# A graph network of six convolutions on one core: the one-hots of a ring's last two edge tiles move to GpSimd, and two small edits

## The chip, the cores and the metric

The kernel runs on one core of a Trainium2 chip. The time is the device time of one execution in microseconds (us), lower is better. One core has five engines that run their own instruction streams and wait for each other by semaphores: TensorE (PE, its weight loads are shown as PEld), VectorE (DVE), ScalarE (ACT), GpSimd (POOL) and SyncE (SP, which here issues nearly all DMAs).

## The reference, cut to what matters

There are 1250 nodes with 512 features and 20000 edges, sorted by dst. Four residual blocks follow one another; each normalizes x, applies a relu, and aggregates over the edges. With them there are six convolutions, called L0, L1A, L1B, L2, L3A and L3B in the kernel.

```python
edge_index = jnp.stack([src, dst])
h = jnp.maximum(_layernorm(x, axis=-1), 0.0)
x = x + relu(mean_of_neighbours(h) @ L0_W_l.T + L0_b_l + h @ L0_W_r.T)           # L0
h = jnp.maximum(_layernorm(x, axis=-1), 0.0)
x = x + sage(relu(sage(h, L1_W1l, L1_b1, L1_W1r)), L1_W2l, L1_b2, L1_W2r)        # L1A, L1B
h = jnp.maximum(_layernorm(x, axis=-1), 0.0)
x = x + layernorm(h + relu(h @ W_self.T + b_self + mean(h[dst] @ W_neigh.T + b_neigh))) * gamma + beta   # L2
h = jnp.maximum(_layernorm(x, axis=-1), 0.0)
x = x + gcn(relu(gcn(h, L3_W1, L3_b1)), L3_W2, L3_b2)                            # L3A, L3B
```

Every aggregation is a sum over the same edges. It can therefore be written as a product with one 1250 x 1250 matrix of edge counts, and that is what the kernel does.

## The kernel before, in words

The nodes are cut in 10 tiles of 128 (NT). The kernel first builds the matrix of counts on TensorE, and then uses it in every convolution.

**Counting, 13 to 138 us.** The edges come in tiles of 128. For a tile, `src_hot` (128 edges x 640) and `dst_hot` (128 edges x 128) are one-hot matrices, 1 where the edge's node equals the column, and the product of the two, summed over edge tiles, is a block of the count matrix. The count matrix is made in 20 windows: b from 0 to 9 and half h from 0 to 1. As the edges are sorted by dst, a window needs only some edge tiles. How many is read at run time from a table (`tiles_of`, through `visits_of`), rounded up to a multiple of RING = 6. One pass over a ring of six edge tiles is called a trip here. Low nodes have more edges, so the first windows take more trips. Each half has its own ring of buffers, `src_hot[h]` and `dst_hot[h]`, with six slots.

In a trip the work is split by slot e:

- DVE (`givers`, line 1197) writes all six `src_hot` (line 1212), and the `dst_hot` of the slots e with BY_ACT <= e < RING - 1, which is slot 4 alone (line 1210). Before slot e it awaits `hot_used[h] >= n + e + 1`, that is, that PE has used this slot in the trip before.
- ACT (`receivers`) writes the `dst_hot` of slots 0 to 3 in two steps: the distance of node and column (`apart`, line 800), then the relu of one minus the distance (line 806).
- GpSimd (`last_receivers`, line 594) writes the `dst_hot` of slot 5. Per window it copies the window's table row into `tab_now` (line 597). Per trip it copies the nodes of the edges in its slot into `key_now` (line 602), awaits that copy, awaits `hot_used[h] >= n + RING`, that is, that PE has used all six slots of the trip before, writes the one-hot (line 607), and awaits its own result.
- PE (`count`, line 1684) multiplies slot by slot, two matmuls of 128 x 320 for each (line 1700), so 12 for a trip. It awaits `first_rows` at slots 0 and 2, `last_rows` at slot 5 and `givers_ready` at each slot, and increments `hot_used` after each slot. Two small matmuls with zeros open a window (line 1690) and one closes it (line 1705). ACT then moves the counts out of PSUM (line 771).

Between the windows PE runs the products of L0: a tile of normalized x is turned (line 1714) and multiplied by the two weights, 12 matmuls each (line 1721, `first_p` and `first_q`). The order on every engine is written out by hand: `merged(b, r)` is followed by `merged_end(b, r)`. For b of 2 to 7 PE has this in a loop of three rounds with two b in each; GpSimd has a loop over b with both halves in it.

**Statistics.** In this stage DVE also makes the mean and variance of a tile of x: `statistics_1` (bn_stats, line 1184), `statistics_2` (bn_aggr into `mv_now`, line 1189) and `statistics_3` (line 1193), a multiplication by 1.0 that moves `mv_now` into the column of `mv` that belongs to the tile.

**The convolutions, from 138 us on.** In each, PE makes the products of the 10 tiles (`products`, line 1721), and then aggregates for 10 receivers i: 20 matmuls of count columns with p_hi and p_lo (line 1814). ACT casts the count columns for receiver i + 2 (`stage`, line 844) when PE is through with receiver i, and DVE combines the result (line 1436), adds it to x, and makes the statistics and the normalized tile of the next convolution. From L1A on these tiles are turned by way of DRAM: DVE transposes 32 x 32 blocks (`square`), SP writes them out (`park`) and reads them back turned into `zT` (`turn`, line 515). ACT makes hT_hi of such a tile (`hi`, line 828), DVE hT_lo (`lo`, line 1236).

ACT works in order, so an `hi` that stands between two casts holds up the second until its DMA has landed. At the end of a convolution, `receive_all` on ACT puts the `hi` of the next convolution's tiles 0 and 1 behind the casts at receivers i = 5 + late // 2 and 6 + late // 2, where late is 2 ahead of L2 and 0 otherwise; DVE has its `lo` at the same i.

```python
def receive(i, staged):
    if staged:
        stage(s, i + 2, i % 2)
    if s + 1 in NORMED:
        deviation(NORMED[s + 1], i)
```

## Time and profile before

| | |
|---|---|
| median of 3 runs | 646.88 us (646.28 to 648.64) |
| profiled execution | 647.0 us |
| span of its trace, first to last instruction | 645.1 us |
| busy: PE / DVE / ACT / POOL | 97% / 62% / 47% / 13% of the span |
| mean granted TensorE clock | 0.997 of full speed |

The profiled execution and the median agree within 0.1 us, so sums made on the trace can be held against the median. The rows that follow come from the profile's page and from views of the trace. Times are us from the start of the span unless marked ns. A row of a group of instructions gives the line, engine, operation, output and inputs and how many there are, then the time busy and the mean of one in ns, then how long the engine sat idle before them and what ended that. A row of a timeline gives the start, the duration, the engine and the line; several instructions in a row are merged in one, with their number behind x, and in square brackets stands the idle time before and what ended it. Matmuls overlap in their records, so the time between the starts says more than a duration.

### The profile page before, as it was taken

The numbers are of one execution on the slowest core, as the hardware profiler recorded it, in microseconds if no ns is written. First come the engines' busy times: TensorE is split into PE (matmuls) and PEld (weight loads), VectorE is DVE, ScalarE is ACT, GpSimd is POOL, SyncE is SP. The second block draws the span as 40 slices with busy tenths as digits, with TensorE's granted clock in tenths as the row PEclk, the third lists the DMA queues.
The fourth block names the chain that finished last, engine by engine and source line by source line (L and its number), as shares of the span: only waits on it lengthen the run. The fifth ranks groups of instructions, "written<-read, shape, count | busy, mean of one in ns | idle before, by whom it ended". The sixth has DMA issues, their size and how long they took to land.

```text
span 645.1 us, 11113 instructions
## 1 busy us (share of the span) xinstructions
PE 626.6 (97%) x3047; PEld 511.2 (79%) x3048; DVE 401.5 (62%) x875; ACT 303.8 (47%) x628; POOL 85.2 (13%) x135
## 2 busy tenths in 40 slices
PE   5989999999989999999999999999999999999997
PEld 4547767777868888888888888888888998899886
DVE  6998999977867434533434888754999730531222
ACT  4887886644423454431224342225478752565210
POOL 4442433200000000000000000000354070000000
PEclk9999999999999999999999999999999999999999
DMA  6300005457684422587550465431200000000102
GB/s 215 117 1 2 1 23 80 63 125 150 105 172 109 109 33 72 142 207 173 122 91 6 130 142 148 98 65 49 81 1 1 1 2 1 2 0 1 49 17 97
DMA packets 151843, 48.39 MB, mean 75 GB/s; under 512 B 133500, under 2 KB 137396, under 8 KB 151800
## 3 DMA queue, kind: packets, MB, share of 16 engines
q1 hardware_dynamic: 150520, 45.34, 30.8%
q10 hardware_dynamic: 1280, 2.56, 1.2%
q8 instruction: 17, 0.28, 0.2%
q14 instruction: 26, 0.21, 0.1%
HBM read 30.44 MB, written 17.44 MB: 74 GB/s over the span
## 4 chain that ended last, share of the span: by engine, by line
PE 86%; DVE 4%; DMA 3%; issue 2%; SPq 2%; ACT 1%; DVEq 1%; ACTq 0%
PE ps L1721 33%; PE ps L1814 23%; PE ps L1851 13%; PE ps L1877 8%; PE ps L1700 8%; DMA count_rows<-count_squares 2%; SPq L491 1%; DVE src_hot L1212 1%; DMA wstage<-in_L_gnn_W_l 1%; PE ps L1714 1%; DVE stats L1184 1%; DVE p_lo L1504 0%; ACT cstage L844 0%; DMA zT<-rows 0%; DVE own L1436 0%
## 5 line engine op out<-in xcount | busy, mean ns | idle before, releaser
L1814 PE MATMUL ps<-p_hi,cstage 128*128 128x512 f32 x400 | 156.0, 390 | 2.8 <-ACT cstage L844 2.8
L1814 PE MATMUL ps<-p_lo,cstage 128*128 128x512 f32 x400 | 155.7, 389 | 0.0
L1721 PE MATMUL ps<-w_hi,hT_hi 128*128 128x512 f32 x320 | 126.3, 395 | 0.6 <-issue 0.4
L1721 PE MATMUL ps<-w_hi,hT_lo 128*128 128x512 f32 x320 | 124.7, 390 | 0.0
L1721 PE MATMUL ps<-w_lo,hT_hi 128*128 128x512 f32 x320 | 124.6, 389 | 0.0
L1814 PEld LDWEIGHTS ps<-p_hi,cstage 128*128 128x128 f32 x400 | 75.1, 188 | 19.7 <-ACT cstage L844 2.9
L1814 PEld LDWEIGHTS ps<-p_lo,cstage 128*128 128x128 f32 x400 | 75.1, 188 | 15.5
L1212 DVE TENSOR_SCALAR src_hot<-iota,nodeT 128x640 bf16<-128x640 f16 x210 | 69.0, 384 | 5.8 <-PE ps L1700 3.7
L1700 PE MATMUL ps<-src_hot,dst_hot 128*128 128x320 bf16 x420 | 65.7, 305 | 5.8 <-DVE src_hot L1212 2.9
L1721 PEld LDWEIGHTS ps<-w_hi,hT_hi 128*128 128x128 f32 x320 | 60.1, 188 | 13.3 <-issue 0.9
L1721 PEld LDWEIGHTS ps<-w_hi,hT_lo 128*128 128x128 f32 x320 | 60.1, 188 | 12.7
L1721 PEld LDWEIGHTS ps<-w_lo,hT_hi 128*128 128x128 f32 x320 | 60.1, 188 | 11.9
L1700 PEld LDWEIGHTS ps<-src_hot,dst_hot 128*128 128x128 bf16 x420 | 36.9, 99 | 28.7 <-DVE src_hot L1212 12.9
L844 ACT CAST cstage<-countT 128x1280 fp32r<-128x1280 uint16 x30 | 37.6, 1263 | 42.7 <-PE ps L1814 40.0
L653 POOL TENSOR_TENSOR x<-x,vec 128x512 f32 (+1 forms) x10 | 13.8, 1387 | 320.8 <-ACT relued L849 320.8
L833 ACT ACTIVATE p_hi<-ps 128x512 fp32r<-128x512 f32 (+1 forms) x40 | 23.8, 596 | 64.5 <-PE ps L1721 64.4
L1242 DVE TENSOR_TENSOR p_lo<-ps,p_hi 128x512 fp32r<-128x512 f32 x40 | 27.5, 689 | 41.7 <-ACT p_hi L833 41.6
L1599 DVE TENSOR_TENSOR u_lo<-ps,u_hi 128x384 fp32r<-128x384 f32 (+1 forms) x24 | 12.5, 585 | 59.3 <-ACT u_hi L957 59.3
L1436 DVE SCALAR_TENSOR_TENSOR own<-ps,nodal,own 128x512 f32<-128x512 f32 x40 | 29.5, 737 | 28.9 <-PE ps L1814 28.9
L946 ACT CAST spans<-countT 128x384 fp32r<-128x384 uint16 (+1 forms) x60 | 31.7, 552 | 33.1 <-PE ps L1851 32.8
L800 ACT ACTIVATE apart<-tab,nodeT 128x128 bf16<-128x128 f16 (+1 forms) x140 | 44.6, 392 | 1.6 <-ACT dst_hot L806 0.4
L1851 PE MATMUL ps<-spans,p_hi 128*128 128x384 f32 (+1 forms) x120 | 42.2, 352 | 0.9 <-issue 0.7
(156 smaller groups left out, 941.3 us busy)
## 6 DMA issues: line engine op xcount, KB each, us to landing
rows<-squares SPq DMA_DIRECT2D x38, 256.0 KB, 2.5
zT<-rows SPq DMA_DIRECT2D x120, 64.0 KB, 2.5
count_rows<-count_squares SPq DMA_DIRECT2D x10, 320.0 KB, 2.2
countT<-count_rows SPq DMA_DIRECT2D x40, 80.0 KB, 3.2
x<-in_x ACTq DMA_DIRECT2D x1, 2304.0 KB
out_x<-x SPq DMA_DIRECT2D x9, 256.0 KB
wstage<-rows SPq DMA_DIRECT2D x32, 64.0 KB, 2.5
wstage<-in_L_gnn_W SPq DMA_DIRECT2D x2, 1024.0 KB, 5.7
```

The lines of the kernel that those rows point to most:

```text
L800: nc.scalar.activation(apart[h][:, e:e + 1, :], tab[:, window(b, h), :], ACT.Abs, scale=-1.0, bias=nodeT[:, 0, bass.ds(t + e, 1)]).then_in ...
L833: nc.scalar.activation(p_hi[:, bass.ds(i, 1), :], ps[:, p_bank(s, r), :], ACT.Copy, scale=1.0 if CONVS[s]["own"] else dis[:, bass.ds(i, 1) ...
L844: nc.scalar.copy(stage_of(s, r), columns(s, i)).then_inc(stage_ready, 1)
L946: nc.scalar.copy(span_of(n % SLOTS, n), span_counts(n)).then_inc(span_ready, 1)
L1212: nc.vector.tensor_scalar(src_hot[h][:, e, :], iota[:, :], nodeT[:, 1, bass.ds(t + e, 1)], None, ALU.is_equal).then_inc(givers_ready[h], 1)
L1242: nc.vector.tensor_tensor(p_lo[:, bass.ds(i, 1), :], ps[:, p_bank(s, r), :], p_hi[:, bass.ds(i, 1), :].bitcast(F32), ALU.subtract).then_in ...
L1436: nc.vector.scalar_tensor_tensor(own_, ps[:, AGG + r:AGG + r + 1, :], scale[:, bass.ds(i, 1)], own_, ALU.mult, ALU.add).then_inc(t_done, 1)
L1700: last = nc.tensor.matmul(ps[:, COUNT + 2 * h + k, 0:NS // 2], dst_hot[h][:, e, :], src_hot[h][:, e, k * (NS // 2):(k + 1) * (NS // 2)], s ...
L1721: last = nc.tensor.matmul(ps[:, bank, :], a[:, r, k, :], w[:, slot, k, :], start=n == 0, stop=n == len(pairs) - 1)
L1814: last = nc.tensor.matmul(ps[:, AGG + r, :], cstage[:, part, k, :], p_[:, k, :], start=n == 1, stop=n == 2 * len(parts) * NT)
L1851: last = nc.tensor.matmul(ps[:, u_bank(l, g) + f, 0:cols], h[:, k, f * P:(f + 1) * P], spans[:, c, 0:cols], start=k == 0 and m == 0, stop= ...
L1877: last = nc.tensor.matmul(ps[:, dense_bank(l, i), :], u[g % 2][:, k, own_], w[:, 0, k, :], start=m == 0, stop=m == len(pairs) - 1)
```

## The change

GpSimd writes the dst_hot of slots 4 and 5, one instruction each, from a key_now of two columns. It still awaits hot_used once for the trip. DVE then writes no dst_hot at all, since BY_ACT <= e < RING - BY_POOL holds for no slot. PE awaits `last_rows` at slot 4 and, with a higher value, at slot 5. The statistics of the counting stage go from bn_aggr to their place in mv directly. And the hi and lo of the next convolution's first two tiles stand at 5 + (s != L1A) and 6 + (s != L1A) where they stood at 5 + late // 2 and 6 + late // 2: for s = L0 that is 6 and 7 where it was 5 and 6; for L1A (5 and 6) and L1B (6 and 7) it is what it was.

```diff
-    BY_ACT = 4
+    BY_ACT, BY_POOL = 4, 2
...
-    mv_now, _ = place("mv_now", [P, 2], F32)
...
-    key_now, _ = place("key_now", [P, 1], F32, place.end)
+    key_now, _ = place("key_now", [P, BY_POOL], F32, place.end)
...
-                    nc.gpsimd.tensor_copy(key_now[:, :], nodeT[:, 0, bass.ds(t + RING - 1, 1)]
+                    nc.gpsimd.tensor_copy(key_now[:, :], nodeT[:, 0, bass.ds(t + RING - BY_POOL, BY_POOL)]
                                           ).then_inc(key_set[h], RING)
                     pool.wait_ge(key_set[h], n + RING)
                     pool.sem_inc(passed_pool, 1)
                     pool.wait_ge(hot_used[h], n + RING)
-                    nc.gpsimd.tensor_scalar(dst_hot[h][:, RING - 1, :], tab_now[:, :], key_now[:, 0:1], None,
-                                            ALU.is_equal).then_inc(last_rows[h], RING)
+                    for k in range(BY_POOL):
+                        nc.gpsimd.tensor_scalar(dst_hot[h][:, RING - BY_POOL + k, :], tab_now[:, :], key_now[:, k:k + 1],
+                                                None, ALU.is_equal).then_inc(last_rows[h], RING // BY_POOL)
                     pool.wait_ge(last_rows[h], n + RING)
...
# ACT, receive_all
-                        if i == 5 + late // 2:
+                        if i == 5 + (s != L1A):
                             first_tile(0)
-                        if i == 6 + late // 2:
+                        if i == 6 + (s != L1A):
                             first_tile(1)
...
# DVE
-                statistics_3(v, i)
...
-                nc.vector.bn_aggr(mv_now[:, :], stats[:, :]).then_inc(aggr_done, 1)
-
-            def statistics_3(v, i):
-                dve.wait_ge(aggr_done, NT * v + i + 1)
-                nc.vector.tensor_scalar(mv[:, bass.ds(i, 1), :], mv_now[:, :].unsqueeze(1), 1.0, None,
-                                        ALU.mult).then_inc(mv_done, 1)
+                nc.vector.bn_aggr(mv[:, i, :], stats[:, :]).then_inc(mv_done, 1)
...
-                        if BY_ACT <= e < RING - 1:
+                        if BY_ACT <= e < RING - BY_POOL:
...
-                        if i == 5 + late // 2:
+                        if i == 5 + (s != L1A):
                             lo(s + 1, 0, 0)
-                        if i == 6 + late // 2:
+                        if i == 6 + (s != L1A):
                             lo(s + 1, 1, 1)
...
# PE, count
-                        if e == RING - 1:
-                            pe.wait_ge(last_rows[h], n + RING)
+                        if e >= RING - BY_POOL:
+                            pe.wait_ge(last_rows[h], n + (e + 1 - (RING - BY_POOL)) * RING // BY_POOL)
```

## Rows read from the trace of the kernel before

**Rows 1.** The page: busy tenths of the span in 40 equal slices.
```profile
PE   5989999999989999999999999999999999999997
...
DVE  6998999977867434533434888754999730531222
```

**Rows 2.** Groups of instructions, 13 to 47.2 us.
```profile
L1700 PEld LDWEIGHTS ps<-src_hot,dst_hot 128*128 128x128 bf16 x156 | 13.1, 102 | 18.5 <-DVE src_hot L1212 11.7 <-issue 1.4 <-POOL dst_hot L607 1.1
L607 POOL TENSOR_SCALAR dst_hot<-tab_now,key_now 128x128 bf16<-128x128 f16 x13 | 11.4, 879 | 8.1 <-PE ps L1700 6.7 <-POOL key_now L602 1.4
...
L1210 DVE TENSOR_SCALAR dst_hot<-tab,nodeT 128x128 bf16<-128x128 f16 x13 | 3.3, 253 | 0.2 <-PE ps L1700 0.2
```

**Rows 3.** Timeline of GpSimd in the first stretch: start, duration, what, idle before.
```profile
22.50 0.19 POOL L602 COPY key_now<-nodeT 128x1 f32 x1 [0.61 <-POOL dst_hot L607]
...
22.96 0.91 POOL L607 TENSOR_SCALAR dst_hot<-tab_now,key_now 128x128 bf16<-128x128 f16 x1 [0.27 <-PE ps L1700]
...
24.95 0.91 POOL L607 TENSOR_SCALAR dst_hot<-tab_now,key_now 128x128 bf16<-128x128 f16 x1 [0.27 <-PE ps L1700]
...
28.05 0.83 POOL L607 TENSOR_SCALAR dst_hot<-tab_now,key_now 128x128 bf16<-128x128 f16 x1 [0.27 <-POOL key_now L602]
...
45.41 0.81 POOL L607 TENSOR_SCALAR dst_hot<-tab_now,key_now 128x128 bf16<-128x128 f16 x1 [0.71 <-PE ps L1700]
```

**Rows 4.** Timeline of DVE: src_hot beside a GpSimd one-hot, and without.
```profile
23.03 1.91 DVE L1212 TENSOR_SCALAR src_hot<-iota,nodeT 128x640 bf16<-128x640 f16 x6
...
61.27 1.28 DVE L1212 TENSOR_SCALAR src_hot<-iota,nodeT 128x640 bf16<-128x640 f16 x4 [0.72 <-PE ps L1700]
```

**Rows 5.** Waits, total, times, longest: 13 to 47.2 us, then 91 to 131.
```profile
POOL dst_hot L607 <- PE ps L1700: 6.7, 8, 1.8
...
POOL dst_hot L607 <- PE ps L1700: 10.8, 6, 2.4
```

**Rows 6.** Timeline of GpSimd in the second stretch and after it.
```profile
62.55 0.93 POOL L607 TENSOR_SCALAR dst_hot<-tab_now,key_now 128x128 bf16<-128x128 f16 x1 [2.25 <-PE ps L1700]
...
65.97 1.30 POOL L607 TENSOR_SCALAR dst_hot<-tab_now,key_now 128x128 bf16<-128x128 f16 x1 [0.27 <-POOL key_now L602]
...
68.76 0.93 POOL L607 TENSOR_SCALAR dst_hot<-tab_now,key_now 128x128 bf16<-128x128 f16 x1 [0.55 <-PE ps L1700]
...
109.98 0.60 POOL L607 TENSOR_SCALAR dst_hot<-tab_now,key_now 128x128 bf16<-128x128 f16 x1 [2.37 <-PE ps L1700]
```

**Rows 7.** Timeline of GpSimd before the counting: two iotas in a row.
```profile
1.22 0.28 POOL L573 IOTA tile_up<- 128x162 f32 x1
1.45 0.28 POOL L575 IOTA tile_dn<- 128x162 f32 x1
```

**Rows 8.** Timeline of PE: counting matmuls, and those that close a window (L1705).
```profile
26.20 0.19 PE L1705 MATMUL ps<-zeros 128*128 128x64 bf16 x1
...
47.12 0.19 PE L1705 MATMUL ps<-zeros 128*128 128x64 bf16 x1
...
60.58 3.42 PE L1700 MATMUL ps<-src_hot,dst_hot 128*128 128x320 bf16 x24
63.84 0.19 PE L1705 MATMUL ps<-zeros 128*128 128x64 bf16 x1
...
93.02 2.20 PE L1700 MATMUL ps<-src_hot,dst_hot 128*128 128x320 bf16 x12
```

**Rows 9.** Timelines of ACT and PE around 184 us.
```profile
184.04 0.63 ACT L828 ACTIVATE hT_hi<-zT 128x512 fp32r<-128x512 f32 x1 [3.67 <-DMA zT<-rows]
184.57 1.24 ACT L844 CAST cstage<-countT 128x1280 fp32r<-128x1280 uint16 x1
...
186.15 0.47 PE L1814 MATMUL ps<-p_hi,cstage 128*128 128x512 f32 x1 [2.48 <-ACT cstage L844]
```

**Rows 10.** The chain of work that ended last: start, us, what; one receiver of L0.
```profile
147.12 4.83 PE ps L1814 x20
```

More of the change, by code:

```diff
@@ L243, in gnn_kernel @@
     coarse_set, exact_set, fine_set = sem("coarse_set"), sem("exact_set"), sem("fine_set")
-    aggr_done = sem("aggr_done")
     scaled_done = sem("scaled_done")
@@ L1305, in _ @@
             statistics_2(0, 0)
-            statistics_3(0, 0)
             split_first(1, range(0, 2))
@@ L1312, in _ @@
             statistics_2(0, 1)
-            statistics_3(0, 1)
             givers(1, 1, found)
@@ L1320, in _ @@
             statistics_2(0, 2)
-            statistics_3(0, 2)
             lo(L0, 1, 1)
@@ L1338, in merged_end @@
                 statistics_2(0, b + 1)
-                statistics_3(0, b + 1)
                 lo(L0, b, r)
```

## Prediction, made before the changed kernel was run

> **What bounds the kernel now.** I read the slices of the span first, then the groups of instructions, the waits of GpSimd, and the timelines of PE and GpSimd. The slices show PE at nine tenths or more from the fifth slice on (one slice dips just after the first), and DVE at seven tenths or more in slices 2 to 11 [rows 1]. So after about 48 us only what makes PE wait counts; before that PE waits for one-hots. The change touches the counting stage (13 to 138 us) and one stretch at 184 us.
>
> In the first 34 us of counting there are 13 trips of the ring, one GpSimd one-hot each. PE's weight loads sat idle 11.7 us until DVE had a src_hot ready and only 1.1 us until GpSimd [rows 2]. This invites the reading "DVE is the bound, GpSimd has room". Its second half has to be tested: GpSimd's one-hots take 11.4 us of the 34, but it also idles around each of its own small copies, and that is no room. Between two one-hots of one window lie 0.61 us until key_now starts, 0.19 of key_now and 0.27 until the one-hot starts: 1.07 [rows 3]. With 0.91 for the one-hot the loop needs 1.98 us a trip, and from 22.96 to 24.95 is 1.99: GpSimd is as close to the limit there as DVE, whose six src_hot take 1.91 and whose dst_hot comes on top [rows 3, 4]. From the last one-hot of a window to the first of the next it needs 28.05 - 25.86 = 2.19 us [rows 3].
>
> Real room is only what GpSimd waited for PE: 6.7 us in 8 waits [rows 5], less the 0.27 that lie before a one-hot in any case, also where nothing from PE is awaited (28.05) [rows 3]: 6.7 - 8 x 0.27 = 4.5 us over 13 trips, or 0.35 a trip.
>
> **What the second one-hot costs GpSimd.** The trace has no two in a row. A lone one, with DVE writing no one-hot at the time, spans 0.60 [rows 6]; beside src_hot the spans are 0.91 and 0.93 [rows 3, 6]; with a DVE dst_hot beside it too, one took 1.30 [rows 6]. Two iotas back to back span 0.28 each but start 0.23 apart [rows 7], so the spacing may be 0.05 less than a span. Bounds: 0.55 and 0.93. In the first stretch I take 0.78, between the ends, since a longer ring trip leaves DVE idle for part of the second one-hot. The wider key_now (two columns for one) is taken at its present 0.19; bounds 0 and 0.05 more a trip, inside those of the one-hot.
>
> **First stretch, 13 to 47 us.** Added are 13 x 0.78 = 10.1 us, less the room of 4.5: GpSimd's last one-hot ends 5.6 later. That one ended at 46.22, and PE's closing matmul came at 47.12, 0.90 behind, because DVE was later still [rows 3, 8]. With GpSimd as the bound, the distance is that of the first window: 25.86 to 26.20, 0.34 [rows 3, 8]. So PE ends **5.6 - 0.6 = 5.0 us later**. With 0.55 it is 7.2 - 4.5 - 0.6 = 2.1; with 0.93, and 0.5 of the room unusable where PE itself is slow (its longest wait was 1.8 [rows 5]), it is 12.1 - 4.0 - 0.6 = 7.5. What DVE saves, 13 dst_hot of 0.25 us [rows 2] and the copies of statistics, buys nothing once GpSimd is the bound. The work of DVE and ACT between windows ends before GpSimd's pair does, since they are through with the last trip's slots before GpSimd begins its second one-hot.
>
> **Second stretch, 47 to 91 us: six windows of two trips.** PE runs 24 matmuls in 3.26 us (60.58 to 63.84, 0.136 each) without a stop [rows 8], trip 2's slots being filled while it eats trip 1's. After the change slots 4 and 5 are both written only once PE has used slot 5 of trip 1, since hot_used is awaited once, for the whole trip. Now the one-hot starts at 62.55 and PE's closing matmul at 63.84, 1.29 later [rows 6, 8]. After: 0.93 + 0.65 + 0.34 = 1.92, **0.63 more**. The second is taken at 0.65 here, near the lone 0.60, because DVE's last src_hot of the window end under the first and statistics follow; with 0.93 it is 0.91 more, with 0.85 and 0.55 it is 0.45 more. Six windows make 3.8. In the two after the loop's turn GpSimd itself will be late for trip 2: before 68.76 it had 0.55 - 0.27 = 0.28 us of room, after a one-hot of 1.30 [rows 6], against about 0.8 added and 0.1 less for want of the dst_hot beside it; I take 0.35 each, bounds 0 and 0.5. Sum **+4.5 us**, bounds 2.7 and 6.5.
>
> **Ten windows of one trip, 91 to 138 us.** GpSimd waited 10.8 us in 6 waits for PE there [rows 5]: 9.2 of room, against 10 second one-hots of 0.6 to 0.9, so PE covers them: 0, at worst 1 us. In the first of these windows 12 matmuls took 2.20 us [rows 8], where 3.42 - 12 x 0.136 = 1.79 is the time without a stop; DVE was late, and with a dst_hot and a copy less (some 0.4 us) this goes: **-0.4 us**. Statistics written straight into mv are off PE's path everywhere else: 0.
>
> **The turned tiles' move.** Only L0's receiving stage changes: ACT's hT_hi of L1A's tile 0 (and DVE's lo) moves from receiver 5 to 6, tile 1's from 6 to 7; for L1A and L1B the old and the new expression agree. ACT waited 3.67 us for the tile's DMA, until 184.04, with the cast of the counts for receivers 8 queued behind (184.57, 1.24 us); PE sat idle 2.48 us for that cast, until 186.15 [rows 9]. After the move the cast starts where that wait began, at 184.04 - 3.67 = 180.37, and ends by 181.7, two us ahead of PE's need at 183.67. Next on ACT's queue behind tile 0's turn is now the cast for receivers 9, from 184.7 to 186.0, and PE wants it after receiver 8's 20 matmuls, which take 4.8 us in the chain [rows 10], so at about 188. SP's order is unchanged. So **-2.5 us**. The lo of tile 0 also no longer holds up DVE; but its transposes for the next tiles then wait more on their DMAs, which may come back as a stop in L1A's products: bounds -2.5 and -1.0.
>
> **Sum** on the profiled execution: 5.0 + 4.5 - 0.4 - 2.5 = +6.6 us, so 647.0 + 6.6 = **653.6 us** (a span of 645.1 with 1.9 around it). The median of the runs, 646.88, differs from it by 0.1. Low ends: 2.1 + 2.7 - 0.4 - 2.5 = +1.9, 648.9. High ends: 7.5 + 6.5 + 1.0 - 0.4 - 1.0 = +13.6, 660.6.
>
> **Rules of the Trainium skill against these rows.** Where six src_hot run with a GpSimd one-hot beside them they take 1.91 us (from 23.03), 0.318 each; four with GpSimd idle take 1.28 (from 61.27), 0.32 each, while GpSimd's own span is 0.91 instead of 0.60 [rows 3, 4, 6]. So GpSimd is held up and DVE is not. The Trainium skill ("SBUF — State Buffer", section "Who interferes with whom") says that a DVE operation in a two-port mode and a GpSimd operation lock each other out, whoever starts second waiting for the whole of the other. The trace agrees on GpSimd's side only; what the other side would give is the rival of that name below. The Trainium skill ("Perfetto Trace Analysis", section "GPSIMD Engine Instruction") also holds that GpSimd's spans are unreliable and that start-to-start spacing is to be used; with the iotas' difference that moves the sum toward its low end.
>
> **Rivals.**
> *GpSimd's room suffices, and the kernel gets faster.* DVE would then stay the bound of the first stretch and lose 13 x 0.25 = 3.3 us: 647.0 - 3.3 - 0.4 - 2.5 = 640.8. For it: the 11.7 us against 1.1 [rows 2]. It decides if the second one-hot takes GpSimd less than 0.35 us of its loop; the shortest row is 0.60. Chance 0.07.
> *The short spacing.* Everything as in my sum with the low ends: 648.9, within 0.5%. For it: the iotas [rows 7], and a DVE that idles more. With cases between it and 650.2 I give it 0.18.
> *Long one-hots.* GpSimd stays beside src_hot all the time, 0.93 or more, and the move's gain is partly given back: 660.6 at the end, 657 in the middle. For it: the 1.30 us that one one-hot took [rows 6], should it be src_hot and not DVE's dst_hot that stretched it. Chance 0.20.
> *DVE is locked out too.* Then a trip costs DVE 6 x 0.318 + 2 x 0.60 = 3.1 us against 2.75 in my GpSimd loop (1.07 + 0.90 + 0.78): 25 x 0.35 = 8.8 more, 662.4. Against it: rows 4. Chance 0.03.
> *The move does nothing* (the wait for turned tiles shows up on PE at the next stage): 656.1. Chance 0.07.
> *My sum*, 651 to 656: 0.45.
>
> **Numbers.** 0.5%, 3.2 us, is about what a measurement of this kernel can tell from no change (its three runs span 2.4 us). Faster than 643.6 takes the first rival: 0.07. Within: 0.18. Slower than 650.2: 0.75. The range leaves out the first rival, what lies beyond the low end and the last 1.6 us before the high end, with DVE locked out: 648.6 to 659.
>
> **What would show it.** In the changed profile: two one-hots in a row per trip on GpSimd, and PE's idle time in counting released by GpSimd instead of DVE; the start-to-start time of first one-hots near 2.75 instead of 1.99 in the first window; counting windows with two trips of some 3.9 us instead of 3.26 on PE; PE without the 2.48 us before the cast of columns 8. The forecast is wrong if two one-hots take GpSimd under 1.3 us, if DVE's src_hot gets longer than 0.38 on average, or if PE stops at the start of L1A's products.

## The result, and the profile after

| | before | after |
|---|---|---|
| median (runs in this comparison) | 646.96 us (7) | 650.91 us (7) |
| extent of the runs | 645.45 to 648.64 | 649.90 to 651.21 |
| profiled execution, its span | 647.0, 645.1 | 651.15, 649.2 |

The ratio is 1.0056, with an interval of 1.0041 to 1.0070: **slower by 4.0 us**, where 6.6 were forecast. It lies in the range, on the side given 0.75.

The page of after first: busy tenths in 40 slices (PE, then DVE), then groups of instructions, then the shares of the chain that ended last.

```profile
PE   6879999999999999999999999999999999999997
...
DVE  6887779877887534443434788754989730541222
...
L1689 PE MATMUL ps<-src_hot,dst_hot 128*128 128x320 bf16 x420 | 69.6, 307 | 9.1 <-POOL dst_hot L606 5.8
...
L1205 DVE TENSOR_SCALAR src_hot<-iota,nodeT 128x640 bf16<-128x640 f16 x210 | 67.9, 387 | 15.5 <-PE ps L1689 13.2
...
L606 POOL TENSOR_SCALAR dst_hot<-tab_now,key_now 128x128 bf16<-128x128 f16 x70 | 51.6, 747 | 20.6 <-PE ps L1689 16.8
...
PE 90%; POOL 4%; DVE 2%; issue 1%; DMA 1%; ACT 1%; ACTq 1%; SPq 0%; DVEq 0%; POOLq 0%
```

DVE is less busy in the first slices than in [rows 1], and now it is PE that DVE waits for: 13.2 us before src_hot. Of the 9.1 us that PE itself idles before its counting matmuls, GpSimd ends 5.8. The mean of a GpSimd one-hot is 747 ns, and there are 70, two for each of 35 trips.

The waits over the whole span in after (total us, times, longest):

```profile
PE ps L1689 <- POOL dst_hot L606: 5.8, 17, 1.2
...
PEld ps L1689 <- DVE src_hot L1205: 14.4, 26, 1.5
...
PEld ps L1689 <- POOL dst_hot L606: 8.3, 18, 0.6
```

The weight loads still seem to wait most for DVE. This is the trap of [rows 2] again, the other way round: DVE itself waits for PE, 13.2 us in the group above, so it isn't what closes the circle. That is seen on the engine that waits for nobody. That is GpSimd, in its timeline of after (start, duration, what, in brackets the idle time before):

```profile
16.95 1.56 POOL L606 TENSOR_SCALAR dst_hot<-tab_now,key_now 128x128 bf16<-128x128 f16 x2 [1.60 <-PE ps L1689]
...
22.14 1.49 POOL L606 TENSOR_SCALAR dst_hot<-tab_now,key_now 128x128 bf16<-128x128 f16 x2 [0.27 <-PE ps L1689]
24.24 0.19 POOL L600 COPY key_now<-nodeT 128x2 f32 x1 [0.61 <-POOL dst_hot L606]
24.69 1.49 POOL L606 TENSOR_SCALAR dst_hot<-tab_now,key_now 128x128 bf16<-128x128 f16 x2 [0.27 <-PE ps L1689]
...
49.34 1.18 POOL L606 TENSOR_SCALAR dst_hot<-tab_now,key_now 128x128 bf16<-128x128 f16 x2 [0.27 <-PE ps L1689]
...
66.64 1.56 POOL L606 TENSOR_SCALAR dst_hot<-tab_now,key_now 128x128 bf16<-128x128 f16 x2 [1.26 <-PE ps L1689]
```

From 22.14 to 24.69 is 2.55 us, where one trip took 1.99 in [rows 3]: the same 1.07 around GpSimd's own copy, and 1.49 for two one-hots in place of 0.91 for one. The 0.27 before each pair is the time that also stands there when nothing is awaited, so GpSimd has no room left in these trips. At 66.64, in the second trip of a window, it does wait for PE.

Where the time went, by stages. The first matmul of counting, the closing matmuls of windows (b, h) and the first aggregation of L0 are starts in PE's timeline:

| start of | before | after | shift |
|---|---|---|---|
| counting | 13.67 | 13.40 | -0.27 |
| closing matmul of (0,0) | 26.20 | 28.76 | +2.56 |
| closing matmul of (1,1) | 47.12 | 50.86 | +3.74 |
| closing matmul of (4,1) | 90.05 | 97.54 | +7.49 |
| closing matmul of (5,0) | 95.05 | 102.16 | +7.11 |
| L0's aggregation | 147.12 | 154.14 | +7.02 |
| L1A's products | 195.55 | 199.59 | +4.04 |
| end of the span | 645.1 | 649.2 | +4.1 |

One thing in the first of these shifts is not the change. In most executions TensorE's granted clock is at the lower of its two levels (1.2 in place of 2.4 GHz) for part of the first microseconds of counting, and its counting matmuls then start 0.27 us apart instead of 0.136. Counting matmuls between 15 and 17 us, in before, in after and in c_after, which is the changed kernel as the experiments have it (us, PE busy with their number, granted clock, DMA share, GB/s):

```profile
15.00:17.00 2.00, 2.00 (x9) 0.50 1.03 392
15.00:17.00 2.00, 2.00 (x9) 1.00 1.05 401
15.00:17.00 2.00, 1.84 (x13) 1.00 1.03 390
```

After has 9 of them as before has, although its row says 1.00; its record of the clock begins only at 17.7 us. From the first to the twelfth start, the matmuls of the first trip take 2.11 us in before, 2.90 in after and 1.50 in c_after.

PE in the second stretch and at the windows' ends in after, which answers to [rows 8]:

```profile
50.86 0.19 PE L1694 MATMUL ps<-zeros 128*128 128x64 bf16 x1
...
64.67 2.88 PE L1689 MATMUL ps<-src_hot,dst_hot 128*128 128x320 bf16 x20
...
67.75 0.95 PE L1689 MATMUL ps<-src_hot,dst_hot 128*128 128x320 bf16 x4 [0.20 <-POOL dst_hot L606]
68.53 0.19 PE L1694 MATMUL ps<-zeros 128*128 128x64 bf16 x1
...
97.54 0.19 PE L1694 MATMUL ps<-zeros 128*128 128x64 bf16 x1
...
100.53 1.79 PE L1689 MATMUL ps<-src_hot,dst_hot 128*128 128x320 bf16 x12
```

The 24 matmuls that ran in 3.26 us before are now broken behind the twentieth, and take 68.53 - 64.67 = 3.86. The twelve of the first one-trip window run in 1.79 us, without their old stop.

ACT in L0's last receivers of after, which answers to [rows 9]:

```profile
187.29 1.25 ACT L843 CAST cstage<-countT 128x1280 fp32r<-128x1280 uint16 x1
...
190.85 0.62 ACT L827 ACTIVATE hT_hi<-zT 128x512 fp32r<-128x512 f32 x1
191.37 1.25 ACT L843 CAST cstage<-countT 128x1280 fp32r<-128x1280 uint16 x1
```

The turned tile's hi no longer waits for its DMA at all, and PE runs through.

### The profile page after: what moved, and what is told of

It is laid out like the page before. It is cut to its first block, busy times and chain, and to the rows that moved or that the text cites. A ratio compares the mean times of both kernels' runs of the same rounds, so it can differ in the third digit from the quotient of the medians.

```text
span 649.2 us, 11033 instructions
## 1 busy us (share of the span) xinstructions
PE 630.0 (97%) x3047; PEld 511.5 (79%) x3048; DVE 394.8 (61%) x830; ACT 304.3 (47%) x628; POOL 106.4 (16%) x170
## 3 DMA queue, kind: packets, MB, share of 16 engines
q10 hardware_dynamic: 1280, 2.56, 1.2%
## 4 chain that ended last, share of the span: by engine, by line
PE 90%; POOL 4%; DVE 2%; issue 1%; DMA 1%; ACT 1%; ACTq 1%; SPq 0%; DVEq 0%; POOLq 0%
PE ps L1710 33%; PE ps L1803 27%; PE ps L1840 13%; PE ps L1866 8%; PE ps L1689 7%; POOL dst_hot L606 4%; PE ps L1703 1%; DMA wstage<-in_L_gnn_W_l 1%; DVE p_lo L1493 0%; PE ps L1661 0%; DVE own L1453 0%; ACTq L425 0%; PE ps L1679 0%; ACT cstage L843 0%; DVE stats L1182 0%
## 5 line engine op out<-in xcount | busy, mean ns | idle before, releaser
L1689 PE MATMUL ps<-src_hot,dst_hot 128*128 128x320 bf16 x420 | 69.6, 307 | 9.1 <-POOL dst_hot L606 5.8
L1205 DVE TENSOR_SCALAR src_hot<-iota,nodeT 128x640 bf16<-128x640 f16 x210 | 67.9, 387 | 15.5 <-PE ps L1689 13.2
L1710 PEld LDWEIGHTS ps<-w_hi,hT_hi 128*128 128x128 f32 x320 | 60.1, 188 | 13.2 <-issue 0.7
L843 ACT CAST cstage<-countT 128x1280 fp32r<-128x1280 uint16 x30 | 37.6, 1263 | 42.7 <-PE ps L1803 40.0
L606 POOL TENSOR_SCALAR dst_hot<-tab_now,key_now 128x128 bf16<-128x128 f16 x70 | 51.6, 747 | 20.6 <-PE ps L1689 16.8
```

The source lines that it names most:

```text
L606: nc.gpsimd.tensor_scalar(dst_hot[h][:, RING - BY_POOL + k, :], tab_now[:, :], key_now[:, k:k + 1], None, ALU.is_equal).then_inc(last_rows ...
L843: nc.scalar.copy(stage_of(s, r), columns(s, i)).then_inc(stage_ready, 1)
L1205: nc.vector.tensor_scalar(src_hot[h][:, e, :], iota[:, :], nodeT[:, 1, bass.ds(t + e, 1)], None, ALU.is_equal).then_inc(givers_ready[h], 1)
L1689: last = nc.tensor.matmul(ps[:, COUNT + 2 * h + k, 0:NS // 2], dst_hot[h][:, e, :], src_hot[h][:, e, k * (NS // 2):(k + 1) * (NS // 2)], s ...
L1710: last = nc.tensor.matmul(ps[:, bank, :], a[:, r, k, :], w[:, slot, k, :], start=n == 0, stop=n == len(pairs) - 1)
```

## The experiments

Two bases carry the experiments. In them and in all that follow, the loaded entry of the table has a stated range, which puts two more instructions of each engine's sequencer in front of a window:

```diff
-            tiles_of[0:1, window(b, h)], engines=[engine.engine], bass_reorder=False)
+            tiles_of[0:1, window(b, h)], engines=[engine.engine], bass_reorder=False,
+            min_val=0, max_val=65535)
```

All ratios are to the kernel before without this line, run on the same chip, with 95% intervals. "First" is the stretch from the first counting matmul to the closing of (1,1), "second" from there to the closing of (4,1), and "receivers" from L0's first aggregation to L1A's products. The three are of one profiled execution each.

| kernel | median, us | ratio | first | second | receivers |
|---|---|---|---|---|---|
| before | 646.96 | 1 | 33.45 | 42.93 | 48.43 |
| after | 650.91 | 1.0056 [1.0041, 1.0070] | 37.46 | 46.68 | 45.45 |
| c_before | 651.09 | 1.0028 [1.0008, 1.0048] | 34.27 | 42.90 | 50.98 |
| c_after | 654.65 | 1.0091 [1.0060, 1.0122] | 38.05 | 46.79 | 45.42 |
| e1_one_hot_back | 645.83 | 0.9956 [0.9938, 0.9974] | 34.76 | 42.77 | 45.44 |
| e2_gpsimd_alone | 659.05 | 1.0155 [1.0118, 1.0193] | 38.86 | 46.84 | 52.21 |
| e3_move_alone | 645.64 | 0.9987 [0.9967, 1.0007] | 35.31 | 42.88 | 45.44 |
| e4_added_alone | 657.78 | 1.0177 [1.0136, 1.0219] | 38.74 | 46.61 | 49.21 |
| e5_slot_4_left_out | 646.68 | 0.9992 [0.9968, 1.0016] | 32.22 | 42.85 | 49.91 |
| e6_wait_for_each | 652.10 | 1.0096 [1.0062, 1.0131] | 38.36 | 46.01 | 45.44 |
| g1_stop_filled | 649.67 | 1.0011 [0.9992, 1.0030] | 34.96 | 43.06 | 49.52 |
| g3_none_on_gpsimd | 646.70 | 0.9964 [0.9942, 0.9985] | 34.91 | 42.72 | 45.44 |
| g4_two_from_third_block | 649.96 | 1.0016 [0.9996, 1.0037] | 32.71 | 47.05 | 45.44 |

Two cautions. The kernel before was timed anew beside each group of experiments (its median was 646.74 us beside one group and 648.99 beside another), so kernels are compared by their ratios. And the first stretch varies by 1 us and more from one execution to the next, mostly by how long PE counts at the lower clock: the matmuls of the first trip take 1.50 us in c_after and g4, 2.0 to 2.5 in before, c_before, e1, e2, e4, e5, e6 and g3, 1.73 and then 2.81 for the second trip in g1, and 2.90 in after and e3, where e3 has 2.67 for the second trip too. With one one-hot on GpSimd, from c_before, e3 and e1, the stretch is 34.27, 35.31 and 34.76. From the closing of (0,0) to that of (1,1), behind that start, it is 21.11, 21.11 and 21.73. The second stretch lies between 42.7 and 43.1 us in every kernel with at most one one-hot on GpSimd and between 46.6 and 47.1 in those with two and one wait, and the receivers without a stop at 45.42 to 45.45, so these are the sharper instrument.

**The two bases.**

> The kernel before, with a range assertion behind each load of a window's table entry (two sequencer instructions on each engine per window), which all experiments have; it is the base for them. The assertions lie between windows, 20 times. If PE is the bound there (after 48 us) they hide; before it four windows may pay 0.1 to 0.2 us each on DVE. Expected 647.0 to 648.0 us.

> The changed kernel with the same assertions. If they cost both kernels the same, it is 4.0 us above c_before, 651 to 652. As GpSimd is on the path between windows until 98 us, its assertions may cost a little more here: up to 5 us above c_before. In the trace: closing matmul of the last two-trip window about 7.5 us later than in c_before.

The stated range costs about 0.3% in each, 1.8 us in c_before where 0 to 1 was expected. The change costs 1.0091 against 1.0028 between them, so its effect is about the same as without the range (1.0056), and the second stretch and the receivers of c_after repeat those of after. The first stretch is 0.6 longer than in after, for two reasons that pull apart: up to the closing of (0,0) it is 1.2 shorter, as PE had the full clock in the first trip, and from there to the closing of (1,1) it is 23.87 us against 22.10. There GpSimd's added instructions lie on its path between windows (from its last pair in (0,0) to the first in (0,1) it needs 2.72 us, from 27.69 to 30.41, where after has 2.38; e2, e4 and e6, with the range too, have 23.75 to 24.02 for the whole), and the granted clock fell once more, from 43.2 to 46.6 us.

**One one-hot given back.** All of the change but its first part:

```diff
-    BY_ACT, BY_POOL = 4, 2
+    BY_ACT, BY_POOL = 4, 1
```

> The changed kernel with BY_POOL = 1: DVE makes slot 4's one-hot again, the move and the statistics stay. Theory (GpSimd's second one-hot is the whole loss, the move the whole gain): PE's closings of the windows fall back to those of before, 7.0 to 7.4 us earlier than in c_after, the move's 3.0 us stays: 3.0 to 3.2 us below c_before, about 644. Rival (the pair costs little by itself and the move or the statistics cost something in the counting): less than 5 us below c_after.

The second stretch falls back from 46.79 to 42.77 us and the first from 38.05 to 34.76. The ratio is 1.3% below c_after's and 0.44% below the kernel before, so the second one-hot on GpSimd is what the change loses by. This version is faster than both, even with the range on it. Against c_before it gains 5.3 us where 3.0 to 3.2 were expected: c_before's receivers took 5.5 us more than e1's, and not 3.0, since its stop of PE was longer and the clock fell behind it.

**GpSimd's part alone, on the kernel before.** The hunks for GpSimd, for PE's waits and for DVE's slot 4 from the change; statistics and the turned tiles stay as they were.

```diff
-                        if BY_ACT <= e < RING - 1:
+                        if BY_ACT <= e < RING - BY_POOL:
...
-                        if e == RING - 1:
-                            pe.wait_ge(last_rows[h], n + RING)
+                        if e >= RING - BY_POOL:
+                            pe.wait_ge(last_rows[h], n + (e + 1 - (RING - BY_POOL)) * RING // BY_POOL)
```

> The kernel before with the GpSimd part alone (slots 4 and 5 on GpSimd), no move, statistics as before. Theory: 7.0 to 7.4 us above c_before, about 654.3; PE's stop of 2.5 us ahead of receiver 8 of L0 is there again. Rival (the loss hangs on the statistics or the move together with it): below 652.

First +4.6 and second +3.9 us against c_before, as forecast within the spread of the first stretch. The time rose by 1.3%, some 8 us, because the receivers also took 1.2 us more than in c_before; the section on the hardware comes back to that.

**The move alone, on the kernel before.**

```diff
-                        if i == 5 + late // 2:
+                        if i == 5 + (s != L1A):
...
-                        if i == 6 + late // 2:
+                        if i == 6 + (s != L1A):
```

> The kernel before with only the move: hi and lo of L1A's first two tiles one receiver later. Theory: PE starts L1A's products 2.5 to 3.0 us earlier and nothing gives it back: about 644.3. Rival (the transposes for the next tiles then wait for their DMAs and stop PE in L1A's products): 646 to 647, with an idle PE before L1721 after 200 us.

The receivers take 45.44 us, the value of every kernel with the move, with no stop of PE there nor at the start of L1A. The ratio falls from 1.0028 to 0.9987, or 0.41% (about 2.7 us; the two intervals just fail to touch). The rival that the stop would come back in the next stage is refuted.

**GpSimd's added time alone.** GpSimd writes a second one-hot into a buffer that nobody reads; DVE keeps slot 4, and PE has its old waits.

```diff
+                    nc.gpsimd.tensor_scalar(spare[:, :], tab_now[:, :], key_now[:, 0:1], None,
+                                            ALU.is_equal).then_inc(last_rows[h], RING // 2)
                     nc.gpsimd.tensor_scalar(dst_hot[h][:, RING - 1, :], tab_now[:, :], key_now[:, 0:1], None,
-                                            ALU.is_equal).then_inc(last_rows[h], RING)
+                                            ALU.is_equal).then_inc(last_rows[h], RING // 2)
```

> The kernel before in which GpSimd makes one further one-hot per trip, into a spare buffer that nobody reads, ahead of its own; DVE still makes slot 4's. It separates what GpSimd pays from what DVE saves. Theory (GpSimd's time is the bound, what DVE saves is worth nothing): as e2, 7 us above c_before, 654. If DVE's saving counts, or the two engines hold each other up: 656 to 658, and src_hot on DVE longer than its mean of 385 ns. If PE's further wait at slot 4 is what costs: it isn't there in this kernel, and the time is near 648.

First +4.5 and second +3.7 against c_before; e2 had +4.6 and +3.9. So the loss needs neither PE's wait at slot 4 nor the missing dst_hot of DVE: GpSimd's time alone makes it. The time itself, 657.78 us, is above the 654 of the theory and within the 656 to 658 of its rival, and src_hot did get longer, 392 ns from 13 to 92 us against c_before's 386. But e2, in which DVE is relieved, has the same two stretches and 390 ns, and its ratio, 1.0155, has an interval that overlaps e4's. If the two engines hold each other up, DVE's part of it is those 6 ns for each src_hot. What DVE saves in e2 is worth nothing that can be seen in these two stretches once GpSimd is the bound.

**Nobody writes slot 4.** On the kernel before. The buffer is filled with zeros once at the start, so the edges of slot 4 are missing from the counts.

```diff
-                        if BY_ACT <= e < RING - 1:
+                        if False:
```

> The kernel before in which nobody makes slot 4's one-hot (it holds zeros from the start, so the edges of slot 4 are left out of the counts); GpSimd makes slot 5's only. It shows what relieving DVE is worth when GpSimd isn't charged for it. The rival of the prediction priced it at 13 x 0.25 = 3.3 us. Theory: GpSimd's loop of 1.98 us in the first window and ACT's of 1.95 stand next to DVE's, so only the starts of windows gain: 1 to 2.5 us below c_before, plus 0.3 at the first one-trip window.

This is the most that the change could have brought by relieving DVE: the first stretch 2.05 us shorter, the second 0.05, the time 0.36% (2.3 us). The rival, 13 x 0.25 = 3.3 us, asked for too much: with one one-hot GpSimd's loop is itself at 1.98 us a trip, and it takes over after the first microseconds won. In e5 no one-hot of GpSimd from 20.98 us to the end of the stretch waits longer than the 0.27 that are always there.

**A wait for each slot.** On c_after: GpSimd awaits slot 4 and slot 5 one by one, and so may begin the pair before PE has used slot 5.

```diff
-                    pool.wait_ge(hot_used[h], n + RING)
                     for k in range(BY_POOL):
+                        pool.wait_ge(hot_used[h], n + RING - BY_POOL + 1 + k)
```

> The changed kernel in which GpSimd awaits slot 4's own release (hot_used of n + 5) before the first one-hot and slot 5's before the second, instead of slot 5's release before both. Theory: in the six two-trip windows after 51 us PE releases GpSimd, so the pair starts 0.27 us earlier (two matmuls) in each: 1.6 us below c_after. In the first four windows GpSimd goes straight from its key to the pair, and nothing changes. Rival (the single wait is the fault of the whole loss): 4 us or more below c_after.

A miss. The second stretch is 0.78 us shorter, half of what was expected, and the ratio is c_after's (1.0096 and 1.0091). The first is 0.31 longer, but that is the clock of its start: from the closing of (0,0) on it is 23.75 us against 23.87. GpSimd's timelines tell why; the same pair first in c_after, then in e6:

```profile
67.66 1.56 POOL L607 TENSOR_SCALAR dst_hot<-tab_now,key_now 128x128 bf16<-128x128 f16 x2 [0.80 <-PE ps L1690]
```

```profile
67.52 1.63 POOL L607 TENSOR_SCALAR dst_hot<-tab_now,key_now 128x128 bf16<-128x128 f16 x2 [0.78 <-PE ps L1690]
...
21.84 1.42 POOL L607 TENSOR_SCALAR dst_hot<-tab_now,key_now 128x128 bf16<-128x128 f16 x2 [0.33 <-PE ps L1690]
```

The pair is longer by 0.07 (the second wait stands inside it), and where GpSimd is the bound the start costs 0.33 in place of 0.27; a trip there still takes 2.54 us, against 2.55 in c_after. The 0.27 us that PE takes over a slot's two matmuls are all that the earlier start can win, and the two waits give back about half of them: 0.78 us over six windows is 0.13 for each.

**None on GpSimd.** On c_after with BY_POOL = 0: GpSimd's part of counting and PE's wait for it are left out, and DVE writes slots 4 and 5.

> The changed kernel with BY_POOL = 0: DVE makes the one-hots of slots 4 and 5, GpSimd none. With e1 (one on GpSimd) and c_after (two) it gives the third point. Theory (with one on GpSimd the two engines are level): DVE is the bound and pays 0.17 to 0.25 us more a trip: the first four windows take 2 to 3 us more than in e1, the six two-trip windows 0 to 1 more; 648 to 650 us. Rival (GpSimd's one-hot already costs more than it saves): the same as e1 or faster, 643 to 646.

A miss too. The second stretch is 42.72 us against e1's 42.77, the first 34.91 against 34.76, and the ratios are 0.9964 and 0.9956. The loss inside a window is there, in DVE's timeline of g3:

```profile
22.61 1.27 DVE L1180 TENSOR_SCALAR src_hot<-iota,nodeT 128x640 bf16<-128x640 f16 x4 [0.16 <-PE ps L1662]
...
24.96 1.27 DVE L1180 TENSOR_SCALAR src_hot<-iota,nodeT 128x640 bf16<-128x640 f16 x4 [0.16 <-PE ps L1662]
```

A trip takes 2.35 us there. With one one-hot on GpSimd and the range it is 2.13 (in c_before and e1, while [rows 3] have 1.99 without the range), so DVE pays 0.22 us more a trip, as expected. But it pays them only in the first window: that one takes 13.71 us against c_before's 13.16, and the three windows after it 21.20 against 21.11. What evens that out is open. From a window's closing matmul to the first counting matmul of the next, the three together take 6.46 us against 6.65, so GpSimd's path from one window to the next is worth 0.2 at most.

e1, on the other side, lost time to a single one-hot in window (0,1). GpSimd's row and the matmul of PE that waited for it:

```profile
32.14 3.03 POOL L607 TENSOR_SCALAR dst_hot<-tab_now,key_now 128x128 bf16<-128x128 f16 x1 [1.47 <-PE ps L1690]
...
35.23 2.34 PE L1690 MATMUL ps<-src_hot,dst_hot 128*128 128x320 bf16 x14 [1.54 <-POOL dst_hot L607]
```

The one-hot spans 3.03 us, to just behind the end of an unbroken run of DVE's instructions from 30.7 to 35.0, and PE idles 1.54 us for it. g1 has the same one at 32.23. Without it e1's first stretch would be shorter, by 1.5 us at most, so GpSimd's first one-hot may be worth 1 to 2 us; the times don't show it.

**Two one-hots from the third block on.** On c_after: GpSimd writes one for b = 0 and 1 and two from b = 2, DVE and PE accordingly.

```diff
+            with pool.Fori(0, 2) as b:
+                for h in range(2):
+                    last_receivers(b, h, 1)
-            with pool.Fori(0, NT) as b:
+            with pool.Fori(2, NT) as b:
...
+                by_pool = 1 if isinstance(b, int) and b < 2 else BY_POOL
```

> The changed kernel with one one-hot on GpSimd in the first four windows and two from the fifth on. It separates the two stretches. Theory (two separate losses that add up): the first stretch falls to that of e1, 3.3 us less than c_after (GpSimd's loop no longer the bound), the second stays at 46.7 to 46.8 us against 42.8 (the pair behind PE's release); 651 us. Rival (the first stretch's delay is what makes the second late): the second stretch falls too, near 43 to 45 us.

The first stretch is that of one one-hot (32.71; 20.63 from the closing of (0,0), against 21.11 in c_before), the second that of two (47.05). The two losses are separate and add up; the one in the second stretch is not the first one carried on. The first stretch is the shortest of all kernels that have one one-hot there and count fully, since in this execution the clock was full from the start. The ratio is 0.7% below c_after's and still above e1's.

**The stop filled.** On c_before: in front of the aggregation for L0's receiver 8, where PE idles, it gets 12 matmuls into a free part of PSUM whose product nobody uses.

```diff
+                        if s == L0:
+                            for _ in range(12):
+                                nc.tensor.matmul(ps[:, COUNT, :], p_hi[:, 0, 0:P], p_hi[:, 0, :],
+                                                 start=True, stop=True)
                         aggregate(NT - 2, 0, parts(0))
```

> c_before, in which PE, ahead of receiver 8 of L0, makes 12 matmuls of 512 columns whose result nobody uses (2.7 us). Without them PE idles there for 2.5 to 3.8 us until ACT's cast, and in c_before, e2, e4 and e5 the granted clock fell to 0.6 to 0.8 of full in the slices right behind, which made L0's receivers take 49.2 to 52.2 us (45.4 with the move). Theory (the move is worth more than the stop, since the idle PE also loses clock): the clock stays at 1.0 behind the stop and the receivers take 45.4 + 3.0 to 4.2 = 48.4 to 49.6 us; time 1 to 2 us below c_before. Rival (the clock falls for another reason): the clock falls there all the same, 50 us or more.

It asks why the receivers of c_before took 50.98 us when those of before took 48.43. PE in both, by windows (us, PE busy with its instructions, granted clock, DMA share, GB/s); first c_before, then g1:

```profile
185.00:190.00 5.00, 1.33 (x5) 0.89 0.69 108
190.00:195.00 5.00, 5.00 (x19) 0.77 0.96 269
```

```profile
185.00:190.00 5.00, 4.20 (x19) 1.00 0.62 99
190.00:195.00 5.00, 4.92 (x21) 1.00 0.81 207
```

With PE kept at work for most of the stop (it still idles 0.89 us) the granted clock stays at 1.00 behind it, and the receivers take 49.52, 1.5 less. In time this is 1.0028 to 1.0011, which the intervals don't separate. For the clock it is a single execution, and in before the clock stayed at 1.00 without the added matmuls, so the cause is made likely and not shown.

## Why the prediction was right, and its sizes too large

**GpSimd has no room: right.** The claim that decided the sign was that [rows 2] mislead and that GpSimd's loop, with the 1.07 us around its key, is already at the limit. e4 shows it with nothing else changed, and g4 shows that it holds stretch by stretch.

**The second one-hot at 0.78 us: 0.59.** This is the term that was mis-sized. In after the 13 pairs of the first stretch span 1.47 us each, where one took 0.879 [rows 2]; the difference is 0.59. The forecast took a middle between 0.55 and 0.93. A lone pair spans 1.18, twice 0.59, so the low end, from the lone one-hot of 0.60 and the iotas, was nearly the whole answer. The reason given for the middle, a DVE idle during part of the second one-hot, isn't what happened: in the trip at 22.14 src_hot runs beside both, and they take 0.76 and 0.74, less than the 0.91 that was at hand for one beside src_hot. Why they are shorter isn't shown. With 0.59 the sum gives 13 x 0.59 = 7.7.

**The room of 4.5 us: 3.2 was used.** GpSimd's waits for PE in the first stretch of after come to 4.6 us in 12, of which 12 x 0.27 are none: 1.3 is left, all of it before the second trip, at 16.95, while PE runs its first trip. That trip ran at the lower clock, 2.90 us for its matmuls. In c_after, where they take 1.50, not one pair of the stretch waits longer than 0.27. So the room that was left is PE's slow start, which the prediction didn't look at; before, too, had the lower clock from 14.5 to 17.9 us, and 1.75 of its 4.5 us of room lie before its second and third one-hots. 7.7 - 3.2 = 4.5 against 4.3 in the rows (the last one-hot's start plus its duration, 45.41 + 0.81 before and 49.34 + 1.18 after). The distance from there to PE's closing matmul is 50.86 - 50.52 = 0.34, as forecast. So +3.7 by the clock of the span (+4.0 from its own start) where 5.0 stood: two errors that partly cancel, one of them the clock's and thus of this execution.

**Second stretch +4.5: +3.75.** The longer end of a window was right. From the pair's start to the closing matmul it is 68.53 - 66.64 = 1.89 us in place of 1.29, and over six windows 1.89 to 2.06, where before had 1.28 to 1.48, so +0.58 to +0.76 against 0.63 forecast. The two windows in which GpSimd should come late for trip 2, 0.35 each, didn't have it. The row that I had was a one-hot of 1.30 with DVE's dst_hot beside it; with that one gone the pairs of trip 1 span 1.18 to 1.62, and every pair of trip 2 starts on PE's release, as at 66.64. The six windows are longer by 0.39 to 0.79, 3.75 in all.

**One-trip windows 0, the first -0.4: right in size, the cause only in part.** It was -0.38, and -0.1 over the other nine. e2, which keeps the statistics' copy, has the first of these windows at 4.61 us against e3's 5.09, and e1, which has no copy but the dst_hot, at 4.90. But e4, in which DVE keeps both, has it at 4.75. So most of the gain comes without any relief of DVE, with the two-trip windows before it that GpSimd lengthens; that DVE gets ahead in them is likely and was not tested. The copies' 0.2 us in that one window is all that was seen of writing statistics to their place.

**The move -2.5: -3.0.** The mechanism was right: receivers 48.43 to 45.45, no stop at L1A's products. The size is larger since PE's idle time of 2.48 us understates its stop: from 183.28, its last matmul before, to 186.15 it is 2.87 us where a step is 0.23, which loses 2.64, and another 0.3 goes in single steps of 0.31 to 0.34 at 186.15, 190.56 and 190.90. The granted clock was 1.00 throughout in before's receivers; the falls that the next section shows are those of other executions. The stop is also the dip of the twelfth slice in [rows 1], which the prediction's "from the fifth slice on" passes over.

**The rivals.** *GpSimd's room suffices* is refuted by e4. *Short spacing* had the right price for the one-hot (0.59 of its 0.55) and so came nearer on the first stretch than my sum did; its 2.7 for the second was too low. *Long one-hots* did not occur in after: the longest pair spans 1.77, the longest single one 1.05. They do occur elsewhere, and the question that this rival left open, src_hot or DVE's dst_hot, is nearly answered by the traces. Sixteen one-hots of GpSimd span 1.27 to 3.03 us, among them one of 1.57 in before at 39.26, which the prediction passed over; they lie in the seven kernels in which DVE writes a dst_hot, each beside one; 100 others that run beside one are shorter. In eleven of the sixteen DVE's dst_hot takes 0.37 or 0.38 us itself, in place of 0.25. In the five in which it writes none (after, c_after, e2, e5, e6) the longest of 315 spans 1.06. *DVE locked out too* did not occur either: src_hot has 387 ns in after and 384 in before, so it was over the 0.38 that was to be a sign against the forecast already before the change. In 13 to 92 us e4, with the most GpSimd work beside a DVE at full load, has 392, c_before 386, and g3, with no one-hot on GpSimd, 380. The Trainium skill ("SBUF — State Buffer", section "Who interferes with whom") describes a lock in both directions for DVE's two-port modes; no view here shows in which mode DVE runs. In these traces GpSimd pays (0.60 alone, 0.91 beside src_hot, 3.03 at worst) and DVE's src_hot some three per cent (392 against 380).

**The sum.** On the spans: -0.27 at the start, +4.0, +3.75, -0.4, -0.1, -3.0 gives +4.0 where +4.1 was read, and the medians differ by 4.0.

What stays open is whether GpSimd's first one-hot is worth having (e1 against g3), and whether a GpSimd loop without the copied key would make room for two. The latter was not tried.

## What to carry to other kernels

Count an engine's loop from start to start, with the gaps around its own small dependent copies, before calling its idle time room; the waits that name another engine are the only room, less what stands before the instruction in any case, and less those for an engine that was slow for a passing reason, as PE was at the start. Work that an engine at its limit is relieved of is worth no more than the distance to the next engine's loop (here some 2 us of 3.3), while work given to the other costs in full. A cheap move that takes a DMA wait out of an in-order queue can be worth more than the work that it is shipped with, and so parts of a change should be timed apart: e1 keeps the move, drops the one-hot, and beats both kernels.

## What the runs showed of the hardware

**PE counts at half speed at first, but not always.** Soon after counting begins the granted clock falls to 0.50 in nine of the thirteen traces, from 14.3 to 15.7 us on until 17.7 to 19.1. In after and e3 the matmuls' spacing shows the lower level from the first one on, until 17.7 and 19.7. Only c_after and g4 start at the full clock throughout. At the lower level the matmuls of 320 columns start 0.27 us apart and not 0.136. Ahead of its first counting matmul PE had idled 1.95 us in before and 1.67 in c_after, so that does not tell the two apart. This alone moves the first trips by up to 1.4 us each, as much as many of the effects looked for here.

**A stop of PE sometimes costs more than itself.** In before the stop of 2.48 us left the granted clock at 1.00. In four others the clock fell in a slice of five microseconds behind it: to 0.77 in c_before (PE idle 3.7 us), 0.58 in e2 (3.8), 0.66 in e4 (1.9) and 0.66 in e5 (2.6). The clearest are e5's rows of PE, start and duration:

```profile
181.82 0.39 PE L1817 MATMUL ps<-p_lo,cstage 128*128 128x512 f32 x1
184.78 0.47 PE L1817 MATMUL ps<-p_hi,cstage 128*128 128x512 f32 x1 [2.57 <-ACT cstage L845]
185.08 0.40 PE L1817 MATMUL ps<-p_lo,cstage 128*128 128x512 f32 x1
185.31 0.52 PE L1817 MATMUL ps<-p_hi,cstage 128*128 128x512 f32 x1
185.63 0.63 PE L1817 MATMUL ps<-p_lo,cstage 128*128 128x512 f32 x1
186.05 0.63 PE L1817 MATMUL ps<-p_hi,cstage 128*128 128x512 f32 x1
186.48 0.63 PE L1817 MATMUL ps<-p_lo,cstage 128*128 128x512 f32 x1
...
188.61 0.51 PE L1817 MATMUL ps<-p_hi,cstage 128*128 128x512 f32 x1
188.96 0.40 PE L1817 MATMUL ps<-p_lo,cstage 128*128 128x512 f32 x1
```

After 2.57 us of idling the matmuls follow each other by 0.23 to 0.32 us, then by 0.43, nearly twice as long, until 188.6: the engine went from 2.4 to 1.2 GHz and back. The eight or so matmuls at the lower level cost about 1.7 us beyond the stop (4.18 from 184.78 to 188.96 for 11 steps, against 11 x 0.227). In all, the receivers took 3.0 us more than 45.44 with the stop in before, and 3.8 to 6.8 in c_before, e2, e4 and e5. A stop of 1.9 us (e4) was followed by a fall and one of 2.5 (before) was not, so its length alone doesn't decide. In no kernel with the move did PE stop or the clock fall among the receivers. What decides is not settled. It also means that the move is worth more than its stop: 3.0 us in the pair that was predicted, 5.5 between c_before and e3's traces, 2.7 between their ratios.

**GpSimd's small operations.** A one-hot of 128 x 128 spans 0.59 to 0.60 us alone, two in a row 1.18, where DVE's takes 0.25. The Trainium skill ("GPSIMD Engine Reference", section "Engine selection") says of elementwise work on GpSimd that "1-input is roughly line-rate"; at this size the rows don't bear it out. Widening key_now to two columns cost nothing (0.24 us in the mean in before and in after, 0.19 in the trips shown). Beside DVE a one-hot takes 0.7 to 1.1 as a rule, and now and then, beside a dst_hot of DVE, 1.3 to 3.0.
